# Mixture-of-experts stage of a fused attention and feed-forward kernel: separate weight signals, later shared additions, four result buffers and a split last gate-up

## The chip, the cores and the metric

One core of a Trainium2 chip runs the whole kernel in one launch. The metric is the device time of one execution in microseconds (us), as the median of several runs. Engines are named as the profile names them: PE (matrix products), ACT (scalar), DVE (vector), POOL (GpSimd) and SP (which issues most of the DMAs).

## What is computed

The kernel computes one transformer layer on 896 tokens (8 sequences of 112) of width 512, in fp32. After a cross-attention block (`x` becomes 896 x 512) comes a feed-forward block:

```python
x = hidden_states.reshape(T, H)
scores = jax.nn.softmax(x @ gate_weight.T, axis=-1)
topk_w, topk_idx = jax.lax.top_k(scores, 2)
combine = jnp.zeros((T, E)).at[jnp.arange(T)[:, None], topk_idx].add(topk_w)
gu = jnp.einsum('th,efh->tef', x, gate_up_weights)        # E = 8 experts, F = 352
act = silu(gu[..., :F]) * gu[..., F:]
y = jnp.einsum('tef,te,ehf->th', act, combine, down_weights)
sgu = x @ shared_gate_up.T                                 # shared expert, Fs = 704
y = y + (silu(sgu[:, :Fs]) * sgu[:, Fs:]) @ shared_down.T
```

The layer's input is added to both blocks' results. Only the two best experts of each token have a weight that isn't zero, so the kernel computes only those.

## The kernel before

**Products in three passes.** A precise fp32 product is made of fast passes: each operand is split into a rounded part `hi` (fp32r) and the remainder `lo`, and a product is hi x lo + lo x hi + hi x hi. ACT copies `hi` (helper `hi`, line 911 in the profile), DVE subtracts to get `lo` (helper `lo`, line 1186). For expert weights this is done anew for every tile, since the split copies of one expert only fit once.

**Shared expert.** It runs in steps j = 0 to 5 over the width Fs (128 columns a step, the last 64), each for tokens t = 0 (4 tiles of 128) and t = 1 (3 tiles). `shared_down` makes the product of one token tile in PSUM bank B, CC, D or A, and DVE adds each into `xres` (`add_shared`, line 1391, semaphore `sres`). The additions of the last step (j = 4, to which the product of step 5 has been added) are seven: four for t = 0, three for t = 1. They run beside the start of the expert stage.

**Routing.** DVE works out the slot of each (token, expert) pair; POOL scatters the rows to `xs_dram` so that each of 21 tiles of 128 rows belongs to one expert. `eid` holds each tile's expert, and every engine reads it with a register load (`value_load`) before it uses the expert's weights.

**Expert stage, tile i = 0 to 20.** In the order of each engine's own instruction list:

- SP: `load_x(i)` fetches the tile's rows to `xs_in` when PE has transposed the tile before (`Tx`). It also writes `xres` to `out` in two pieces (`start_sum`, line 362): tiles 0 to 4, and tiles 5 and 6 once all seven last additions are done. Both landings, with an older one, make `ysum0` reach 48. The lists of the weight DMAs are SP's too: 8 gate-up loads and the first down loads, signalled by `we`, and the last three experts' down loads, by `we_late`.
- PE: `gate_up(i)`, 24 products (line 837) in four chunks of the contraction; `t_x(i + 1)`, 4 transposes (line 737); `down(i - 1)`, 6 split products (line 524, semaphore `edn_split`) and the plain rest (line 854, `edn`); `t_act(i)`, 3 transposes of the activation (line 876). `down(i - 1)` waits for `ey` of the tile before it, as both use bank A. The last tile's down product (`last_down`, line 865) is plain, in two column parts.
- ACT: the next tile's first three `gu_hi`, `silu(i)`, `xs_hi(i + 1)`, the fourth `gu_hi`, `dn_hi(i)`, `put_y(i - 1)` (line 1116: bank A times the routing weight to `y_sb`), `put_actT(i)`. Before all this ACT waits for `we` and for the last shared gate-up. For the last tile the order is `silu`, `put_last_actT`, `put_y(19)`, `put_last_y`.
- DVE: two `gu_lo` of the next tile, `expert_act(i)` (line 1499), `xs_lo(i + 1)`, two more `gu_lo`, `dn_lo(i)`, `aT_lo(i)`; ahead of the loop the `gu_lo` of tile 0, each followed by one shared addition, then two more; the seventh addition follows in i = 0.
- POOL: `dn_hi1(i + 1)` (line 493: the second half of the down weights' `hi`, allowed once `edn_split` says that the earlier down product has read the buffer), then the scatter-add of tile i's result to `out` (line 505). Scatter i waits for `ey`, and for `yst` = 16 i, so for the landing of scatter i - 1; scatter 0 waits for `ysum0` = 48 as well. Two `y_sb` buffers: `put_y(i)` waits for the landing of scatter i - 2.

Of the kernel before, what the change touches and what calls it, by code (L numbers as in the profile page):

```python
# [5 lines left out]
ACT = mybir.ActivationFunctionType  # L6
# [6 lines left out]
P = 128  # L13
# [29 lines left out]
def build(nc, x, ctxT, wqT, wkvT, woT, gateT, guT, dnT, sguT, sdnT, out):  # L43
# [118 lines left out]
    actT_plain = m.inside(loop, "actT_plain", [P, P])  # L162
    act_last = nc.alloc_sbuf_tensor_at("act_last", [P, len(FK), P], F32, offset=x2T_at)
    y_sb = [m.inside(loop, f"y_sb{i}", [P, H]) for i in range(2)]

    parts = [shared_at, shared_end]
    gu_parts = m.inside(parts, "gu_parts", [P, C, 2, 2 * F], F32R)
# [56 lines left out]
    def ring_parts(b):  # L224
# [6 lines left out]

    names = (

        "x0 xt1 xt2 xrest wq0 wq1 wq2 wq3 wkeys wvals wo wgate ctx0 ctx1 wsg0 wsg1 wsd0 wsd1 wsd2 we we_late "

        "const zt sel zero wgpad sumg idf "

# [15 lines left out]
    with nc.Block() as block:  # L253
# [3 lines left out]
        def _(sp):  # L257
# [42 lines left out]
            def load_gu(e, sem):  # L300
                sp.dma_start(w_gu[:, e * GU:(e + 1) * GU], guT[e].rearrange("p c f -> p (c f)")).then_inc(sem, 16)
# [24 lines left out]
                sp.dma_start(xs_in[:, 0:H], xs_dram[bass.ds(i * P, P), 0:H]).then_inc(s["xin"], 16)  # L326

            for e in range(0, 2):
                load_gu(e, s["we"])
            next_sd(2)  # L330
            next_sg(2)
            for e in range(2, 5):
                load_gu(e, s["we"])
            next_sg(3)
            next_sd(3)
            for e in range(5, E):
                load_gu(e, s["we"])
            for e in range(n_early):
                load_dn(e, s["we"])
            next_sd(5)  # L340
            next_sg(4)
            next_sd(4)
# [4 lines left out]
            sp.wait_ge(s["ysum0"], 16)  # L347
            load_x(0)
            for e in range(n_early, E - n_late):
                load_dn(e, s["we"])  # L350
            sp.dma_start(dest[:, :, :], xs_dram[:, H:H + 2].bitcast(U32).rearrange("(n p) o -> p n o", p=P),
                         allow_slow_non_contiguous=True).then_inc(s["dest"], 16)
            sp.wait_ge(s["sg"], NBLK * NJ)
            for e in range(E - n_late, E):
                load_dn(e, s["we_late"])


            sp.wait_ge(s["Tx"], 1)
# [6 lines left out]
            start_sum(0, BLK + 1)  # L365
            sp.wait_ge(s["Tx"], 2)
            load_x(2)
            sp.wait_ge(s["sres"], NX * ND)
            start_sum(BLK + 1, NX)
            with sp.Fori(3, NT) as i:  # L370
                sp.wait_ge(s["Tx"], i)
                load_x(i)

# [5 lines left out]
        def _(pool):  # L379
# [102 lines left out]
            scatter(1, "scat2")  # L482

            pool.wait_ge(s["pos"], 3)
            pool.wait_ge(s["we"], 16 * (3 * E - 2 * n_late))
            pool.wait_ge(s["we_late"], 16 * 2 * n_late)
            pool.wait_ge(s["sdn"], NX * ND)

            def dn_hi1(i):
                e = pool.value_load(eid[0:1, i:i + 1], min_val=0, max_val=E - 1)  # L490
                if i >= 1:
                    pool.wait_ge(s["edn_split"], i)
                pool.tensor_copy(dn2[0][:, 1, :], w_dn[:, bass.ds(e * DN + H, H)]).then_inc(s["dn_hi1"], 1)  # L493

            dn_hi1(0)
            for i in range(NT):
                if i + 1 < NT - 1:
                    dn_hi1(i + 1)
                if i == 0:
                    pool.wait_ge(s["dest"], 16)  # L500
                    pool.wait_ge(s["ysum0"], 16 * 3)
                pool.wait_ge(s["ey"], i + 1)
                if i >= 1:
                    pool.wait_ge(s["yst"], 16 * i)
                pool.indirect_dma_start(  # L505
                    out=out[:, :], out_offset=bass.IndirectOffsetOnAxis(ap=dest[:, i, 0:1], axis=0),
                    in_=y_sb[i % 2][:, :], in_offset=None, compute_op=ALU.add).then_inc(s["yst"], 16)


        @block.tensor  # L510
        def _(pe):
# [372 lines left out]
            gate_up(1)  # L884
            t_x(2)
            pe.wait_ge(s["pos"], 3)
            pe.wait_ge(s["we"], 16 * (3 * E - 2 * n_late))
            pe.wait_ge(s["we_late"], 16 * 2 * n_late)
            down(0, expert(0))
            t_act(1)  # L890
            with pe.Fori(2, NT - 1) as i:
# [4 lines left out]
                down(i - 1, e)  # L896
                t_act(i)
            e_last = [expert(i) for i in (NT - 2, NT - 1)]
            gate_up(NT - 1)
            pe.wait_ge(s["ey"], NT - 2)  # L900
            down(NT - 2, e_last[0])
            t_act(NT - 1)
            fill_with_transposes(S[2], 5)
            pe.wait_ge(s["sres"], NX * ND)
            last_down(NT - 1, e_last[1])

# [2 lines left out]
        def _(act):  # L909
# [201 lines left out]
            def put_y(i):  # L1111

                act.wait_ge(s["edn"], i + 1)
                if i >= 2:
                    act.wait_ge(s["yst"], 16 * (i - 1))
                act.activation(y_sb[i % 2][:, :], A[:, :], ACT.Copy, scale=dest[:, i, 1:2].bitcast(F32))\  # L1116
                    .then_inc(s["ey"], 1)

            def put_last_y(i):
                act.wait_ge(s["yst"], 16 * (i - 1))  # L1120
                for n, (bank_, at, width) in enumerate(last_parts):
                    act.wait_ge(s["edn"], i + 1 + n)
                    ins = act.activation(y_sb[i % 2][:, at:at + width], bank_[:, 0:width], ACT.Copy,
                                         scale=dest[:, i, 1:2].bitcast(F32))
                ins.then_inc(s["ey"], 1)

# [8 lines left out]
                act.activation(actT_plain[0:w, :], B[0:w, 2 * P:3 * P], ACT.Copy).then_inc(s["aT"], 1)  # L1135

            act.wait_ge(s["pos"], 3)
            act.wait_ge(s["we"], 16 * (3 * E - 2 * n_late))

            act.wait_ge(s["sg"], NBLK * NJ)  # L1140
            e = expert(0)
# [3 lines left out]
            for i in range(NT):  # L1145
                if i + 1 < NT:
                    e_next = expert(i + 1)
                    for c in range(C - 1):
                        gu_hi(e_next, i + 1, c)
                if i == NT - 1:  # L1150
                    silu(i)
                    put_last_actT(i)
                    put_y(i - 1)
                    break
                silu(i)
                xs_hi(i + 1)
                gu_hi(e_next, i + 1, C - 1)
                if i == 0:
                    act.wait_ge(s["sdn"], NX * ND)
                    act.wait_ge(s["we_late"], 16 * 2 * n_late)  # L1160
                    act.wait_ge(s["dest"], 16)
                dn_hi(e, i)
                if i >= 1:
                    put_y(i - 1)
                put_actT(i)
                e = e_next
# [4 lines left out]
        def _(dve):  # L1171
# [333 lines left out]
            for c in range(C):  # L1505
                if c == 2:
                    xs_lo(0)
                gu_lo(e, 0, c)
                add_shared(ND - 1, 0, c, c + 1)
            add_shared(ND - 1, 1, 0, 2)  # L1510
            for i in range(NT):
                if i + 1 < NT:
                    e_next = expert(i + 1)
                    for c in range(2):
                        gu_lo(e_next, i + 1, c)
                expert_act(i)
                if i + 1 < NT:
                    xs_lo(i + 1)
                    for c in range(2, C):
                        gu_lo(e_next, i + 1, c)  # L1520
                    dn_lo(e, i)
                    aT_lo(i)
                else:
                    dve.wait_ge(s["Ta"], i + 1)
                    w = FK[2][1]
                    dve.tensor_copy(act_last[0:w, 2, :], B[0:w, 2 * P:3 * P]).then_inc(s["aT_last"], 1)
                if i == 0:
                    add_shared(ND - 1, 1, 2)
                e = e_next

# [33 lines left out]
```

## Time and profile before

| what | value |
|---|---|
| median of 3 runs | 351.81 us (350.88 to 352.39) |
| the profiled execution, its own time | 353.07 us |
| span of that profile | 351.3 us |
| PE busy | 332.9 us (95%) |
| DVE busy | 271.6 us (77%) |
| ACT busy | 230.0 us (65%) |
| POOL busy | 118.5 us (34%) |
| granted clock of PE, mean | 0.992 of full speed |

The profile is one execution. Times in it count from its first instruction. A timeline row gives start, duration, engine, line, operation, result <- operands, shape and count; in square brackets stands how long the engine had been idle before it, and which instruction (or DMA) ended that idle time. The chain of work that ended last is followed back from the last instruction, each step to what released it. "SPq", "ACTq" and the like are an engine's instruction queue, as opposed to its datapath. Busy times of matrix products are modelled at their ends, so consecutive rows of PE overlap a little: the distance between starts is what to read.

### The profile page before, as it was taken

How to read it: one execution, taken by the hardware profiler on the slowest of the kernel's cores; microseconds unless marked ns; L12 is line 12 of the kernel's file. 1: busy time of each engine (PE TensorE's matmuls, PEld its weight loads, DVE VectorE, ACT ScalarE, POOL GpSimd, SP SyncE). 2: the span in 40 equal slices, each digit the busy share in tenths (PEclk: the TensorE clock that was granted, in tenths of full speed). 3: DMA queues.
4: the chain of work that ended last, by engine and by line, in shares of the span. 5: the costliest groups of instructions: out<-in, count | busy, mean ns of one | idle time of the engine just before them, and what ended most of it. 6: DMA issues, size and time to landing. Idle time of an engine off the chain costs nothing.

```text
span 351.3 us, 7091 instructions
## 1 busy us (share of the span) xinstructions
PE 332.9 (95%) x2281; PEld 280.5 (80%) x2282; DVE 271.6 (77%) x464; ACT 230.0 (65%) x586; POOL 118.5 (34%) x136
## 2 busy tenths in 40 slices
PE   6999989999999999999999999999999999999980
PEld 6898877777776797988897878898889889988860
DVE  4798978999946258835586998999899899989900
ACT  3577899999973233213235578888888888888720
POOL 3332753555541000256200033343244234324411
PEclk9999999999999999999999999999999999999996
DMA  7999100000003799993599735434443543444233
GB/s 253 368 349 380 64 3 2 3 2 2 2 2 108 284 331 387 400 355 129 169 292 246 261 101 86 93 60 72 82 88 60 82 92 67 67 82 91 30 41 49
DMA packets 29051, 49.47 MB, mean 141 GB/s; under 512 B 7136, under 2 KB 12256, under 8 KB 28000
## 3 DMA queue, kind: packets, MB, share of 16 engines
q1 hardware_dynamic: 24880, 39.91, 35.0%
q0 software_dynamic: 4144, 9.23, 15.0%
q8 instruction: 13, 0.21, 0.3%
q14 instruction: 14, 0.11, 0.1%
HBM read 32.22 MB, written 16.92 MB: 140 GB/s over the span
## 4 chain that ended last, share of the span: by engine, by line
PE 54%; ACT 14%; DVE 10%; DMA 9%; issue 5%; POOL 4%; SPq 1%; POOLq 1%; ACTq 0%; DVEq 0%
PE bank L837 22%; PE bank L524 19%; ACT prob L956 8%; PE bank L854 5%; POOL xs_dram L474 4%; DMA xs_dram<-x2n,slot_i 3%; DMA w_dn<-dnT 3%; PE bank L708 2%; PE bank L876 2%; ACT probT L911 2%; PE bank L737 1%; DMA out<-y_sb,dest 1%; DVE xres L1391 1%; DMA w_sg<-sguT 1%; DMA ctx<-ctxT 1%
## 5 line engine op out<-in xcount | busy, mean ns | idle before, releaser
L1186 DVE TENSOR_TENSOR gu_parts<-w_gu,gu_parts 128x704 fp32r<-128x704 f32 x84 | 78.9, 972 | 1.7 <-ACT gu_parts L911 1.6
L911 ACT ACTIVATE gu_parts<-w_gu 128x704 fp32r x84 | 66.2, 794 | 18.4 <-PE bank L837 17.2
L837 PE MATMUL bank<-gu_parts,xsT_hi 128*128 128x352 f32 x336 | 69.5, 328 | 0.8 <-DVE xsT_lo L1186 0.8
L837 PEld LDWEIGHTS bank<-gu_parts,xsT_hi 128*128 128x128 f32 x336 | 55.6, 189 | 1.6 <-issue 1.2
L493 POOL CAST dn_hi<-w_dn 128x512 fp32r x20 | 19.7, 984 | 101.0 <-PE bank L524 69.0
L505 POOL DMA_INDIRECT out<-y_sb,dest x21 | 33.3, 1585 | 22.9 <-ACT y_sb L1116 17.2
L837 PE MATMUL bank<-gu_parts,xsT_lo 128*128 128x352 f32 x168 | 40.9, 325 | 0.0
L524 PE MATMUL bank<-x2T_hi,w_sg_lo 128*128 128x512 f32 (+1 forms) x88 | 32.6, 371 | 0.3
L524 PE MATMUL bank<-x2T_hi,w_sg_hi 128*128 128x512 f32 (+1 forms) x88 | 32.0, 363 | 0.0
L524 PE MATMUL bank<-x2T_lo,w_sg_hi 128*128 128x512 f32 (+1 forms) x88 | 31.9, 363 | 0.0
L837 PEld LDWEIGHTS bank<-gu_parts,xsT_lo 128*128 128x128 f32 x168 | 29.3, 189 | 0.0
L911 ACT ACTIVATE act_s_hi<-act_s 128x512 fp32r<-128x512 f32 (+1 forms) x10 | 5.8, 578 | 32.4 <-DVE act_s L1371 20.2
L474 POOL DMA_INDIRECT xs_dram<-x2n,slot_i x14 | 14.3, 1019 | 37.1 <-DVE eid L1471 33.1
L1186 DVE TENSOR_TENSOR dn_lo<-w_dn,dn_hi 128x1024 fp32r<-128x1024 f32 x20 | 24.6, 1228 | 0.8 <-POOL dn_hi L493 0.8
L956 ACT ACTIVATE prob<-score,negmax 112x112 f32<-112x112 f32 x64 | 24.1, 411 | 0.0
L956 ACT ACTIVATE prob<-bank,negmax 112x112 f32<-112x112 f32 x64 | 21.8, 363 | 1.9 <-DVE negmax L1231 1.9
L1391 DVE TENSOR_TENSOR xres<-xres,bank 128x512 f32<-128x512 f32 x35 | 22.0, 677 | 0.0
L854 PE MATMUL bank<-w_dn,actT_plain 96*128 x40 | 20.5, 592 | 0.0
L524 PEld LDWEIGHTS bank<-x2T_hi,w_sg_lo 128*128 128x128 f32 x88 | 16.5, 188 | 4.9 <-issue 2.5
L1499 DVE TENSOR_TENSOR act_e<-bank,silu_e 128x352 f32<-128x352 f32 x21 | 11.0, 523 | 11.8 <-ACT silu_e L1109 11.8
L911 ACT ACTIVATE probT<-bank 112x448 f32<-112x448 f32 x32 | 16.6, 554 | 3.9 <-PE bank L708 3.9
L404 POOL TENSOR_TENSOR prob<-prob,rrow 112x448 f32<-112x448 f32 x16 | 14.7, 931 | 11.7 <-DVE rrow L1235 11.7
(196 smaller groups left out, 804.9 us busy)
## 6 DMA issues: line engine op xcount, KB each, us to landing
w_gu<-guT SPq DMA_DIRECT2D x8, 1408.0 KB, 9.7
xs_dram<-no_row SPq DMA_DIRECT2D x1, 5460.0 KB, 19.2
xs_in<-xs_dram SPq DMA_DIRECT2D x21, 256.0 KB, 2.6
w_dn<-dnT SPq DMA_DIRECT2D x8, 512.0 KB, 6.2
w_sg<-sguT SPq DMA_DIRECT2D x10, 256.0 KB, 5.6
w_dn<-dnT SPq DMA_DIRECT2D x8, 192.0 KB, 6.7
w_sd<-sdnT SPq DMA_DIRECT2D x5, 256.0 KB, 4.8
out<-xres SPq DMA_DIRECT2D x1, 1280.0 KB, 5.4
```

Of the source, the lines that this page charges most:

```text
L404: pool.tensor_tensor(prob[r][:, :, :], prob[r][:, :, :], rrow[:, r, :].unsqueeze(2).to_broadcast([SQ, C, SQ]), ALU.mult)\
L474: pool.indirect_dma_start(out=xs_dram[:, :], out_offset=bass.IndirectOffsetOnAxis(ap=slot_i[:, k, n:n + 1], axis=0), in_=x2n[:, n, :], in_ ...
L493: pool.tensor_copy(dn2[0][:, 1, :], w_dn[:, bass.ds(e * DN + H, H)]).then_inc(s["dn_hi1"], 1)
L505: pool.indirect_dma_start(out=out[:, :], out_offset=bass.IndirectOffsetOnAxis(ap=dest[:, i, 0:1], axis=0), in_=y_sb[i % 2][:, :], in_offse ...
L524: ins = pe.matmul(dst, a, b, start=start and n == 0, stop=stop and n == len(passes) - 1)
L837: ins = pe.matmul(dst[:, 0:F], xsT[x_][:, c, :], gu2[w_][:, c, f0:f0 + F], start=c == 0 and n == 0, stop=c == C - 1 and n == 2)
L854: pe.matmul(A[:, :], actT_plain[0:w, :], w_dn[0:w, bass.ds(e * DN + 2 * H, H)], start=False, stop=True).then_inc(s["edn"], 1)
L911: act.activation(dst, src, ACT.Copy).then_inc(s[sem], 1)
L956: ins = act.activation(prob[r][:, c, :], src, ACT.Exp, bias=negmax[:, r, c:c + 1], accum_out=rowsum[:, r, c:c + 1])
L1186: dve.tensor_tensor(lo_, src, hi_.bitcast(F32), ALU.subtract).then_inc(s[sem], 1)
L1391: dve.tensor_tensor(xres[:, n, :], xres[:, n, :], (B, CC, D, A)[i][:, :], ALU.add)\
L1499: dve.tensor_tensor(act_e[:, :], S[1][:, 0:F], silu_e[:, :], ALU.mult).then_inc(s["eact"], 1)
```

## The change

1. The semaphores `we` and `we_late` become `wegu` (gate-up loads), `wedn` and `wedn_late` (down loads). ACT waits only for `wegu` ahead of the stage, and for the down loads ahead of its first `dn_hi`. POOL's wait for the down weights and the shared product moves behind its first register load.
2. DVE: ahead of the loop each shared addition comes before its `gu_lo`, not after it; one addition follows instead of two; the last two are made in i = 1 and i = 2, behind `aT_lo(i)`, instead of one in i = 0. SP's second `start_sum` moves behind `load_x(4)` accordingly.
3. Four `y_sb` buffers (the new two lie where `act_s0` was). POOL's list now runs `dn_hi1` two tiles ahead of the scatter for i below 4: dn 0, 1, 2, scatter 0, dn 3, scatter 1, dn 4, scatter 2, dn 5, scatter 3, scatter 4, dn 6, scatter 5, dn 7, and so on, one ahead.
4. Last tile: `gate_up(20)` is cut in two halves of two chunks with `down(19)` between them; 8 filling transposes follow it and 4 (before: 5) follow `t_act(20)`; ACT makes `put_y(19)` ahead of `silu(20)`.

```diff
@@ SP
-            for e in range(0, 2):
-                load_gu(e, s["we"])
+                load_gu(e, s["wegu"])
...
             for e in range(n_early, E - n_late):
-                load_dn(e, s["we"])
+                load_dn(e, s["wedn"])
...
-                load_dn(e, s["we_late"])
+                load_dn(e, s["wedn_late"])
...
             load_x(2)
+            for i in (3, 4):
+                sp.wait_ge(s["Tx"], i)
+                load_x(i)
             sp.wait_ge(s["sres"], NX * ND)
             start_sum(BLK + 1, NX)
-            with sp.Fori(3, NT) as i:
+            with sp.Fori(5, NT) as i:
@@ POOL
-            pool.wait_ge(s["we"], 16 * (3 * E - 2 * n_late))
-            pool.wait_ge(s["we_late"], 16 * 2 * n_late)
-            pool.wait_ge(s["sdn"], NX * ND)
             def dn_hi1(i):
                 e = pool.value_load(eid[0:1, i:i + 1], min_val=0, max_val=E - 1)
-                if i >= 1:
+                if i == 0:
+                    pool.wait_ge(s["wedn"], 16 * 2 * (E - n_late))
+                    pool.wait_ge(s["wedn_late"], 16 * 2 * n_late)
+                    pool.wait_ge(s["sdn"], NX * ND)
+                else:
                     pool.wait_ge(s["edn_split"], i)
...
             dn_hi1(0)
+            dn_hi1(1)
             for i in range(NT):
-                if i + 1 < NT - 1:
-                    dn_hi1(i + 1)
+                ahead = 2 if i < NY else 1
+                if i != NY and i + ahead < NT - 1:
+                    dn_hi1(i + ahead)
...
-                    in_=y_sb[i % 2][:, :], in_offset=None, compute_op=ALU.add).then_inc(s["yst"], 16)
+                    in_=y_sb[i % NY][:, :], in_offset=None, compute_op=ALU.add).then_inc(s["yst"], 16)
@@ PE
-            gate_up(NT - 1)
+            gate_up(NT - 1, range(C // 2))
             pe.wait_ge(s["ey"], NT - 2)
             down(NT - 2, e_last[0])
+            gate_up(NT - 1, range(C // 2, C))
+            fill_with_transposes(S[2], 8)
             t_act(NT - 1)
-            fill_with_transposes(S[2], 5)
+            fill_with_transposes(S[2], 4)
@@ ACT
-                if i >= 2:
-                    act.wait_ge(s["yst"], 16 * (i - 1))
+                if i >= NY:
+                    act.wait_ge(s["yst"], 16 * (i - NY + 1))
...
-            act.wait_ge(s["we"], 16 * (3 * E - 2 * n_late))
+            act.wait_ge(s["wegu"], 16 * E)
...
                 if i == NT - 1:
+                    put_y(i - 1)
                     silu(i)
                     put_last_actT(i)
-                    put_y(i - 1)
...
                     act.wait_ge(s["sdn"], NX * ND)
-                    act.wait_ge(s["we_late"], 16 * 2 * n_late)
+                    act.wait_ge(s["wedn"], 16 * 2 * (E - n_late))
+                    act.wait_ge(s["wedn_late"], 16 * 2 * n_late)
@@ DVE
+                add_shared(ND - 1, 0, c, c + 1)
                 gu_lo(e, 0, c)
-                add_shared(ND - 1, 0, c, c + 1)
-            add_shared(ND - 1, 1, 0, 2)
+            add_shared(ND - 1, 1, 0, 1)
...
-                if i == 0:
+                if i == 1:
+                    add_shared(ND - 1, 1, 1, 2)
+                if i == 2:
                     add_shared(ND - 1, 1, 2)
```

## Rows read from the trace of the kernel before

**Rows 1.** Chain of work that ended last, one tile of the expert loop.

```profile
214.97 3.89 PE bank L837 x24
...
219.15 1.47 PE bank L524 x6
...
221.81 3.89 PE bank L837 x24
```

**Rows 2.** The same chain, what it stands on where the stage starts.

```profile
178.32 9.49 DMA w_dn<-dnT
```

**Rows 3.** Timeline of ACT, start of the stage.

```profile
186.97 0.53 ACT L911 ACTIVATE act_p<-silu_s 64x384 fp32r<-64x384 f32 x1 [0.74 <-DVE silu_s L1371]
188.74 2.83 ACT L911 ACTIVATE gu_parts<-w_gu 128x704 fp32r x4 [1.25 <-DMA w_dn<-dnT]
...
198.08 0.47 ACT L1109 ACTIVATE silu_e<-bank 128x352 f32<-128x352 f32 x1
```

**Rows 4.** Timeline of PE, start of the stage.

```profile
190.47 0.46 PE L737 MATMUL bank<-ident_f,xs_in 128*128 128x128 f32 x4
191.44 0.47 PE L524 MATMUL bank<-w_sd_hi,act_s_lo 128*128 128x512 f32 x1 [0.51 <-DVE xres L1391]
...
194.00 0.81 PE L837 MATMUL bank<-gu_parts,xsT_hi 128*128 128x352 f32 x4
...
200.02 0.88 PE L837 MATMUL bank<-gu_parts,xsT_hi 128*128 128x352 f32 x4
...
207.91 0.89 PE L837 MATMUL bank<-gu_parts,xsT_hi 128*128 128x352 f32 x4 [0.77 <-DVE xsT_lo L1186]
```

**Rows 5.** Timeline of DVE, start of the stage.

```profile
198.81 0.51 DVE L1499 TENSOR_TENSOR act_e<-bank,silu_e 128x352 f32<-128x352 f32 x1
199.25 0.68 DVE L1186 TENSOR_TENSOR xsT_lo<-bank,xsT_hi 128x512 fp32r<-128x512 f32 x1
...
202.35 1.23 DVE L1186 TENSOR_TENSOR dn_lo<-w_dn,dn_hi 128x1024 fp32r<-128x1024 f32 x1 [0.83 <-POOL dn_hi L493]
...
203.82 0.68 DVE L1391 TENSOR_TENSOR xres<-xres,bank 128x512 f32<-128x512 f32 x1
```

**Rows 6.** Stretch of one tile: length; PE, PEld, DVE, ACT, POOL busy; clock, DMA.

```profile
214.74:221.57 6.83, 6.83 (x43) 6.00 (x40) 6.30 (x9) 5.75 (x11) 2.63 (x3) 1.00 0.44 77
```

**Rows 7.** Timeline of SP, the second write of xres.

```profile
204.53 0.39 SPq L362 DMA_DIRECT2D out<-xres x1
```

**Rows 8.** Timeline of POOL in the expert stage.

```profile
206.07 0.61 POOL L493 CAST dn_hi<-w_dn 128x512 fp32r x1 [3.87 <-PE bank L524]
208.29 1.94 POOL L505 DMA_INDIRECT out<-y_sb,dest  x1 [1.61 <-DMA out<-xres]
...
220.80 1.04 POOL L493 CAST dn_hi<-w_dn 128x512 fp32r x1 [3.56 <-PE bank L524]
...
332.06 1.56 POOL L505 DMA_INDIRECT out<-y_sb,dest  x1 [0.64 <-ACT y_sb L1116]
...
344.92 1.54 POOL L505 DMA_INDIRECT out<-y_sb,dest  x1 [4.13 <-DMA out<-y_sb,dest]
```

**Rows 9.** The instructions of line 505, their landings.

```profile
DMA to landing us min/median/max: 4.4/4.9/5.4
```

**Rows 10.** Chain of work that ended last, scatter 19.

```profile
339.24 4.93 DMA out<-y_sb,dest
```

**Rows 11.** Timeline of all engines, last two tiles.

```profile
331.09 0.69 ACT L1116 ACTIVATE y_sb<-bank,dest 128x512 f32<-128x512 f32 x1
...
331.30 0.88 PE L837 MATMUL bank<-gu_parts,xsT_hi 128*128 128x352 f32 x4
...
333.23 0.41 DVE L1186 TENSOR_TENSOR actT_split_lo<-bank,actT_split_hi 128x256 fp32r<-128x256 f32 x1
...
337.48 0.49 PE L876 MATMUL bank<-ident,act_e 128*128 128x128 f32 x3
...
340.86 0.98 ACT L1123 ACTIVATE y_sb<-bank,dest 128x384 f32<-128x384 f32 x2 [1.89 <-PE bank L865]
```

More of the change, by code:

```diff
@@ L164, in build @@
     y_sb = [m.inside(loop, f"y_sb{i}", [P, H]) for i in range(2)]
+    y_sb += [nc.alloc_sbuf_tensor_at(f"y_sb{i + 2}", [P, H], F32, offset=act0_at + 4 * H * i) for i in range(2)]
+    NY = len(y_sb)
     parts = [shared_at, shared_end]
@@ L232, in build @@
     names = (
-        "x0 xt1 xt2 xrest wq0 wq1 wq2 wq3 wkeys wvals wo wgate ctx0 ctx1 wsg0 wsg1 wsd0 wsd1 wsd2 we we_late "
+        "x0 xt1 xt2 xrest wq0 wq1 wq2 wq3 wkeys wvals wo wgate ctx0 ctx1 wsg0 wsg1 wsd0 wsd1 wsd2 wegu wedn wedn_late "
         "const zt sel zero wgpad sumg idf "
@@ L332, in _ @@
             for e in range(2, 5):
-                load_gu(e, s["we"])
+                load_gu(e, s["wegu"])
             next_sg(3)
@@ L336, in _ @@
             for e in range(5, E):
-                load_gu(e, s["we"])
+                load_gu(e, s["wegu"])
             for e in range(n_early):
-                load_dn(e, s["we"])
+                load_dn(e, s["wedn"])
             next_sd(5)
@@ L349, in _ @@
             for e in range(n_early, E - n_late):
-                load_dn(e, s["we"])
+                load_dn(e, s["wedn"])
             sp.dma_start(dest[:, :, :], xs_dram[:, H:H + 2].bitcast(U32).rearrange("(n p) o -> p n o", p=P),
@@ L886, in _ @@
             pe.wait_ge(s["pos"], 3)
-            pe.wait_ge(s["we"], 16 * (3 * E - 2 * n_late))
-            pe.wait_ge(s["we_late"], 16 * 2 * n_late)
+            pe.wait_ge(s["wedn"], 16 * 2 * (E - n_late))
+            pe.wait_ge(s["wedn_late"], 16 * 2 * n_late)
             down(0, expert(0))
@@ L1113, in put_y @@
                 act.wait_ge(s["edn"], i + 1)
-                if i >= 2:
-                    act.wait_ge(s["yst"], 16 * (i - 1))
-                act.activation(y_sb[i % 2][:, :], A[:, :], ACT.Copy, scale=dest[:, i, 1:2].bitcast(F32))\
+                if i >= NY:
+                    act.wait_ge(s["yst"], 16 * (i - NY + 1))
+                act.activation(y_sb[i % NY][:, :], A[:, :], ACT.Copy, scale=dest[:, i, 1:2].bitcast(F32))\
                     .then_inc(s["ey"], 1)
             def put_last_y(i):
-                act.wait_ge(s["yst"], 16 * (i - 1))
+                act.wait_ge(s["yst"], 16 * (i - NY + 1))
                 for n, (bank_, at, width) in enumerate(last_parts):
                     act.wait_ge(s["edn"], i + 1 + n)
-                    ins = act.activation(y_sb[i % 2][:, at:at + width], bank_[:, 0:width], ACT.Copy,
+                    ins = act.activation(y_sb[i % NY][:, at:at + width], bank_[:, 0:width], ACT.Copy,
                                          scale=dest[:, i, 1:2].bitcast(F32))
```

## The prediction

> **What bounds the kernel now.** I read the chain of waits first, then the timelines of the engines where the chain leaves PE. From tile 3 of the expert stage on the chain stands on PE alone [rows 1]: a gate-up of 3.89 us, from whose start it is 219.15 - 214.97 = 4.18 to the down product (gate-up and `t_x`), and 221.81 - 214.97 = 6.84 to the next gate-up. Over one tile PE is busy for all of 6.83 us, DVE for 6.30, ACT 5.75, POOL 2.63 [rows 6]. No edit shortens a product, so a gain can only come from the two ends of the stage.
>
> At its start the chain stands on the last early down-weight load, which lands at 178.32 + 9.49 = 187.81 [rows 2]; ACT issued its last shared piece at 186.97, and makes the first gate-up weights at 188.74 [rows 3]. PE then stands 0.51 us for DVE's first shared addition, and before gate-up 2, at 207.91, for DVE's `xsT_lo` [rows 4]. At the end two scatters run one after the other: scatter 19 starts at 339.24 and lands 4.93 us later [rows 10], scatter 20 starts at 344.92 [rows 8] and the span ends at 351.3, so 6.38 behind the last scatter's start.
>
> I call G(i) the start of gate-up i. Before: G(0) 194.00, G(1) 200.02, G(2) 207.91 [rows 4], G(20) 331.30 [rows 11].
>
> **Part 1, signals and additions: PE leads by 1.78 us at G(2).** ACT no longer waits for the down weights. Landing to first `gu_hi` was 188.74 - 187.81 = 0.93 (register load included); from the last shared issue at 186.97 that makes 187.90, 0.84 earlier [rows 2, 3]. The first addition no longer stands behind `gu_lo`, so it needs only PE's product, and PE runs on from 190.47 + 0.46 = 190.93 where it resumed at 191.44 [rows 4]. The addition that the next product needs, and `xs_lo(0)`, come forward with ACT's copies, so I carry the 0.51: G(0) = 193.49.
>
> G(1) waits for `xs_lo(1)`. `silu(0)` starts 198.08 - 194.00 = 4.08 behind G(0), so at 197.57; it takes 0.47. In the old run DVE was late to its `act_e` because of the additions ahead of it; now `act_e` can start at 198.08, 0.51 behind `silu`, and `xs_lo(1)` 199.25 - 198.81 = 0.44 later, at 198.52. From there to the gate-up was 200.02 - 199.25 = 0.77, so G(1) = 199.29, 0.73 earlier [rows 3, 4, 5].
>
> G(2) would have been 200.02 + 6.84 = 206.86 had nothing waited; it was 207.91, so 1.05 is the loss there. DVE was late through its wait of 0.83 for POOL's half of the weights, and the addition at 203.82, 0.68 long [rows 5]. POOL's register load now runs before its wait, and the addition is gone from this tile. Together with the 0.73 that is 2.2 us, more than the 1.05, so PE is not stopped: G(2) = 199.29 + 6.84 = 206.13, a gain of 1.78. The other bound is 0.51 alone (a second hold that I don't see takes the rest). I take 1.78, since each wait in it is named by a row.
>
> The two additions now fall in tiles where DVE is busy 6.30 of 6.83 [rows 6]. 0.53 is free, and an addition is 0.68 long with about 0.08 of overlap: 0.6. The excess of 0.07 twice is covered, as DVE's results lie ahead of their use: `aT_lo` starts 333.23 - 331.30 = 1.93 behind the gate-up start and is needed at 4.18 [rows 1, 11]. SP's two extra unrolled loads are the loop's own, and PE's split wait is for loads that landed before; both cost nothing. What `start_sum` at about 215.9 has behind it in SP's list, `load_x(5)`, is due only at G(3) + 4.18 = 217.2.
>
> **Part 2, the scatters start late, and POOL's list makes PE pay 2.12 us.** This is where I differ from what the four buffers seem to promise. Scatter 0 needs all of `xres` in `out`. The last addition was at 203.82, SP wrote at 204.53, scatter 0 began at 208.29: 4.47 behind the addition [rows 5, 7, 8]. Now the last addition comes behind `aT_lo(2)`: G(3) = 212.97, plus 1.93, plus 0.33 for `aT_lo` = 215.23. Scatter 0 starts at 219.70, 11.4 later.
>
> `yst` makes a scatter wait for the landing of the one before. Landing to next start was 344.92 - (339.24 + 4.93) = 0.75 [rows 8, 10]; a landing takes 4.9 in the median, 4.4 to 5.4 [rows 9]. I give the first 5.4, since it also issued for 1.94 and not 1.56 [rows 8], and the rest 4.9: scatter 1 at 225.85, then 5.65 each, 231.50, 237.15, and scatter 4 at 242.80, done issuing at 244.37. In PE's rhythm scatters are 6.84 apart, so the backlog shrinks by only 1.19 a tile and lasts until about scatter 10. `put_y` never waits for it: `put_y(4)`, at about 233, needs the landing of scatter 0 at 225.1.
>
> `dn_hi1` does wait. `dn 3` became ready at 220.80 [rows 8], now 1.78 earlier, 219.02, but stands behind scatter 0, until 221.64. It then meets an idle DVE and takes 0.61, as at 206.07, not 1.04 [rows 8]. `dn_lo` takes 1.14 up to the next start, `aT_lo` 0.41 [rows 11], so down 3 may run at 223.9; due is G(4) + 4.18 = 223.99. Not late, with 0.1 to spare. `dn 4` and `dn 5`, behind scatters 1 and 2, are ready when POOL is free within 1.6 us: covered. `dn 6` stands behind scatter 4: 244.37 + 0.05 + 0.61 + 0.05 + 1.14 + 0.41 = 246.63 for down 6, due at G(7) + 4.18 = 206.13 + 34.20 + 4.18 = 244.51. PE stands for 2.12 us. `dn 7`, behind scatter 5, is within its slack again.
>
> On the price of that cast: the steady one takes 1.04 beside a DVE subtraction [rows 8]. The Trainium skill (SBUF — State Buffer, "Who interferes with whom") says that a DVE instruction with two SBUF inputs and a GpSimd one that reads SBUF exclude each other in turn. The two durations agree with it; with 1.04 the stall would be 2.55.
>
> The unknown here is the scatters' spacing while they queue. From the shortest landing of 4.4, scatter 4 starts 1.5 earlier and 0.6 of the stall is left; from 5.4 for all, 3.6. I take the median row.
>
> **Part 3, the last tile: 1.10 us gained.** All is 0.34 late now (2.12 - 1.78): G(20) = 331.64. Two chunks take half of 3.89, but down 19 needs `aT_lo(19)`: 333.23 + 0.34 + 0.41 + 0.05 = 334.03, a stall of 0.44, better than the 3.89 that it waited for. Down 19 took 337.48 - (331.30 + 3.89) = 2.29 [rows 1, 11], so it ends at 336.32 and the second half at 338.27. `silu` starts 0.19 behind (4.08 - 3.89), 338.46; 0.51 later `act_e`, 0.51 long [rows 5]; 0.04 behind that `t_act(20)`: 339.52, where it was 337.48 [rows 11]. The eight transposes lie inside this wait. So the last result, ready at 340.86 + 0.98 = 341.84, comes 2.04 later, 343.88, and lets scatter 20 start 0.28 behind it (as 332.06 behind 331.09 + 0.69 [rows 8, 11]), at 344.16. The other input, scatter 19: y(19) would let it go at about 337.5, but scatter 18 starts at 332.06 + 0.34 [rows 8], lands 4.93 and lets go 0.75 later, 338.08; so scatter 20 could start at 343.76. The later one is 344.16, against 344.92 before: -0.76, of which this part is -1.10. Without the stall of part 2 it would be -2.88. Bounds of this part: nothing, if `put_y(19)` is late for a reason that I don't see, and 1.5 (to 343.76).
>
> **Sum.** -1.78 + 2.12 - 1.10 = -0.76. The profiled execution took 353.07, 1.26 above the median of the runs; what is added and taken away has the same length in both, so from 351.81 it is 351.0 us.
>
> **Rivals.**
> *The backlog costs nothing.* Landings queue closer than I read them, or POOL's late half is needed later. Then -2.88: 348.9; with 0.6 of stall left, 349.5. For it: only one pair of scatters back to back was traced. Against it: that pair measures 4.93 + 0.75, and it is the quiet end of the kernel. The Trainium skill (DMA: Bandwidth & Descriptors, "Anatomy of one DMA") gives a GpSimd-issued DMA 2.0 us plus its bytes at 436 GB/s, an estimate of 2.6 us for 256 KB; by that rule the backlog would be gone by scatter 3 and this rival would hold. The traced 4.9 speaks against it. 29%.
> *The late start costs twice, and the change is slower.* At `dn 3` I have 0.1 us to spare. If the second write of `xres` and what follows takes longer than 4.47, each us of it stops PE at down 3, while the stall at down 6 remains, since both its times move along. Slower by over 0.5% needs 2.6 us there: scatter 0 at 222.3. At 3 us the sum is -0.76 + 2.9 = +2.1: 353.9. For it: POOL's wait for that write was the only one it had, and the loads of rows share the queue. Against it: the write is smaller than the first piece, and alone. 9%.
> *The front gains less*, 0.51 only: +0.5, 352.3. Part of my case's range.
>
> **How the numbers follow.** 0.5%, about what a measurement of this kernel can tell from no change, is 1.76 us. My forecast, a mid-stage stall between 1.1 and 3.6 and a front gain between 0.5 and 1.8, has 62% and gives 350.0 to 352.6; it lies within 0.5% nearly wholly. Faster takes the first rival and the edge of mine: 0.31. Slower 0.09, same 0.60. The range reaches down to the case without a stall, 348.8, and up to 352.9.
>
> **What would show it.** Right: G(2) near 206.1, no PE wait by DVE there; scatter 0 at 219 to 220; scatters 5.65 apart until about scatter 9; one PE gap of about 2 us before down 6, with DVE's `dn_lo` waiting for POOL; down 19 between the halves, scatter 20 released by ACT. Wrong: no gap near 244 (first rival); a gap near 224 as well (second); G(2) later than 207.

## The result, and the profile after

The changed kernel takes 356.06 us in the median of 4 runs (355.38 to 356.13), the kernel before 351.96 (350.88 to 352.39) beside it: ratio 1.0108, 95% interval 1.0079 to 1.0137. It is slower by 4 us where I forecast 0.8 us less, and it lies outside my range of 348.8 to 352.9.

First the waits in the expert stage of the changed kernel: who waited for what, in total us, how often, and the longest.

```profile
POOL out L513 <- DMA out<-y_sb,dest: 23.9, 8, 4.1
...
POOL out L513 <- DMA out<-xres: 6.4, 1, 6.4
...
DVE dn_lo L1197 <- POOL dn_hi L499: 5.8, 2, 3.6
...
PE bank L845 <- issue: 2.4, 4, 1.0
```

Eight scatters waited for the landing of the one before, where only the last did before, and DVE waited 5.8 us in two places for POOL's half of the down weights. The timeline of POOL gives the order (answers to [rows 8]; line 513 is the scatter, 499 the cast `dn_hi1`):

```profile
212.04 1.12 POOL L499 CAST dn_hi<-w_dn 128x512 fp32r x1 [5.60 <-PE bank L532]
219.57 2.31 POOL L513 DMA_INDIRECT out<-y_sb,dest  x1 [6.41 <-DMA out<-xres]
221.28 1.21 POOL L499 CAST dn_hi<-w_dn 128x512 fp32r x1
225.70 1.59 POOL L513 DMA_INDIRECT out<-y_sb,dest  x1 [3.20 <-DMA out<-y_sb,dest]
...
231.41 1.58 POOL L513 DMA_INDIRECT out<-y_sb,dest  x1 [2.90 <-DMA out<-y_sb,dest]
...
237.78 2.04 POOL L513 DMA_INDIRECT out<-y_sb,dest  x1 [2.85 <-DMA out<-y_sb,dest]
243.90 1.55 POOL L513 DMA_INDIRECT out<-y_sb,dest  x1 [4.08 <-DMA out<-y_sb,dest]
244.89 1.19 POOL L499 CAST dn_hi<-w_dn 128x512 fp32r x1
```

`dn 3` runs behind scatter 0, at 221.28; `dn 6` behind scatter 4, at 244.89. On DVE the two that wait for them:

```profile
222.64 1.23 DVE L1197 TENSOR_TENSOR dn_lo<-w_dn,dn_hi 128x1024 fp32r<-128x1024 f32 x1 [2.27 <-POOL dn_hi L499]
...
246.22 1.23 DVE L1197 TENSOR_TENSOR dn_lo<-w_dn,dn_hi 128x1024 fp32r<-128x1024 f32 x1 [3.56 <-POOL dn_hi L499]
```

And PE (answers to [rows 4]; line 845 is the gate-up, 745 the transposes `t_x`, 532 the down product):

```profile
189.74 0.46 PE L745 MATMUL bank<-ident_f,xs_in 128*128 128x128 f32 x4
...
192.38 0.80 PE L845 MATMUL bank<-gu_parts,xsT_hi 128*128 128x352 f32 x4
...
197.16 0.54 PE L745 MATMUL bank<-ident_f,xs_in 128*128 128x128 f32 x4 [0.82 <-DMA xs_in<-xs_dram]
...
227.83 0.89 PE L845 MATMUL bank<-gu_parts,xsT_hi 128*128 128x352 f32 x4 [0.61 <-issue]
...
247.98 0.47 PE L532 MATMUL bank<-dn_hi,actT_split_lo 128*128 128x512 f32 x1 [1.25 <-DVE dn_lo L1197]
251.76 0.88 PE L845 MATMUL bank<-gu_parts,xsT_hi 128*128 128x352 f32 x4 [0.96 <-issue]
```

"issue" as the end of an idle time means that the profile shows no instruction and no DMA that PE waited for. What stood there is the matter of e3.

To compare kernels I cut each profile at the transposes `t_x`, one set per tile: from t_x(0) to t_x(3) is the stage's start, from t_x(3) to t_x(20) the middle (17 tiles, 116.3 if nothing waits), from t_x(20) to the end of the span the end. What differs before t_x(0) is not the change's: that code is the same, yet t_x(0) falls between 189.3 and 191.7 us in these profiles. Each row is one profiled execution; the ratio is of many runs. us:

| kernel | start | middle | end | ratio to before, 95% interval |
|---|---|---|---|---|
| before | 21.39 | 116.41 | 23.03 | |
| changed | 20.20 | 122.03 | 22.23 | 1.0108 (1.0079 to 1.0137) |
| e1 additions early | 20.17 | 117.57 | 22.07 | 1.0008 (0.9984 to 1.0032) |
| e2 two ahead up to 11 | 21.71 | 118.87 | 22.15 | 1.0045 (1.0021 to 1.0069) |
| e3 register load later | 20.78 | 121.91 | 22.51 | 1.0126 (1.0090 to 1.0163) |
| e4 last tile only | 21.15 | 116.21 | 22.28 | 0.9992 (0.9968 to 1.0016) |
| e5 early, one ahead | 19.89 | 116.43 | 22.42 | 0.9969 (0.9950 to 0.9989) |
| e6 e5 and rows first | 25.56 | 116.37 | 22.12 | 1.0115 (1.0097 to 1.0133) |
| e8 e6 and register later | 24.65 | 116.27 | 22.24 | 1.0083 (1.0059 to 1.0108) |
| e9 e5 and register later | 19.46 | 116.28 | 22.11 | 0.9939 (0.9913 to 0.9964) |
| e10 signals only | 20.03 | 116.41 | 22.54 | 0.9988 (0.9967 to 1.0009) |

The start ends behind G(2). The changed kernel gains 1.19 there and 0.80 at the end and loses 5.62 in the middle: +3.6, where the medians lie 4.1 apart. The other 0.5 us is less than what executions of one kernel differ by (the profiled execution of before took 353.07 where its median is 351.96), and how much one row of this table can be off by is seen in e4 and e10. The loss has an address. Distances between successive `t_x`, read from the timelines of PE, us:

| from, to | 4, 5 | 5, 6 | 6, 7 | 7, 8 | 8, 9 | 9, 10 | 10, 11 |
|---|---|---|---|---|---|---|---|
| before | 6.84 | 6.84 | 6.84 | 6.94 | 6.87 | 6.84 | 6.84 |
| changed | 6.83 | 8.05 | 7.40 | 7.10 | 9.44 | 7.60 | 7.10 |
| e1 | 6.93 | 6.88 | 6.83 | 6.84 | 7.43 | 7.52 | 6.83 |
| e2 | 6.84 | 8.05 | 6.83 | 7.00 | 6.87 | 7.19 | 6.84 |
| e3 | 6.84 | 7.40 | 6.84 | 6.84 | 11.92 | 6.83 | 6.84 |
| e5 | 6.85 | 6.84 | 6.84 | 6.95 | 6.87 | 6.83 | 6.85 |

The stretch 5, 6 holds down 3, which needs `dn 3`, and 8, 9 holds down 6. Over 6.84, the first group of three stretches loses 1.21 + 0.56 + 0.26 = 2.03, the second 2.60 + 0.76 + 0.26 = 3.62.

### The profile page after: what moved, and what is told of

Its sections match the earlier page's. It is cut to its first block, busy times and chain, and to the rows that moved or that the text cites. A ratio compares the mean times of both kernels' runs of the same rounds, so it can differ in the third digit from the quotient of the medians.

```text
span 354.2 us, 7094 instructions
## 1 busy us (share of the span) xinstructions
PE 335.3 (95%) x2288; PEld 282.7 (80%) x2289; DVE 272.6 (77%) x464; ACT 230.9 (65%) x586; POOL 121.8 (34%) x136
## 4 chain that ended last, share of the span: by engine, by line
PE 60%; ACT 12%; DMA 12%; DVE 7%; issue 5%; POOL 1%; POOLq 1%; SPq 0%; DVEq 0%
PE bank L532 32%; PE bank L845 16%; ACT prob L966 8%; DMA out<-y_sb,dest 7%; PE bank L862 4%; DMA xs_in<-xs_dram 2%; PE bank L716 2%; ACT probT L921 2%; PE bank L884 1%; PE bank L745 1%; DMA w_sg<-sguT 1%; DVE prob L1250 1%; DVE xnT_lo L1197 1%; DMA ctx<-ctxT 1%; DMA out<-xres 1%
## 5 line engine op out<-in xcount | busy, mean ns | idle before, releaser
L513 POOL DMA_INDIRECT out<-y_sb,dest x21 | 35.0, 1665 | 45.6 <-DMA out<-y_sb,dest 23.9
L499 POOL CAST dn_hi<-w_dn 128x512 fp32r x20 | 23.0, 1151 | 78.3 <-PE bank L532 48.8
L532 PE MATMUL bank<-dn_hi,actT_split_lo 128*128 128x512 f32 x40 | 17.3, 434 | 1.8 <-DVE dn_lo L1197 1.2
## 6 DMA issues: line engine op xcount, KB each, us to landing
xs_dram<-no_row SPq DMA_DIRECT2D x1, 5460.0 KB, 19.2
```

The costliest lines, as they stand in the source:

```text
L513: pool.indirect_dma_start(out=out[:, :], out_offset=bass.IndirectOffsetOnAxis(ap=dest[:, i, 0:1], axis=0), in_=y_sb[i % NY][:, :], in_offs ...
L532: ins = pe.matmul(dst, a, b, start=start and n == 0, stop=stop and n == len(passes) - 1)
```

## Experiments

### e1: the last additions back in their old places

```diff
-            add_shared(ND - 1, 1, 0, 1)
+            add_shared(ND - 1, 1, 0, 2)
...
-                if i == 1:
-                    add_shared(ND - 1, 1, 1, 2)
-                if i == 2:
+                if i == 0:
                     add_shared(ND - 1, 1, 2)
```

SP's second `start_sum` goes back behind `load_x(2)`.

> The changed kernel with one part undone: the last shared additions are made where the kernel before made them (two ahead of the loop, the seventh in tile 0), and SP writes the second piece of xres before it fetches row tile 3. Theory (the late additions hold scatter 0 back, and POOL's in-order list then hands PE its down weights late at down 3 and down 6, which costs 5.6 us by the trace): scatter 0 starts near 208, no DVE wait for POOL's half of the weights beyond tile 0, G(20) - G(2) = 18 x 6.84 = 123.1 instead of 128.9, and with the addition back in tile 0 G(2) up to 1 us later; in all 5 to 5.6 us less than the changed kernel, so 350.5 to 351.1. Rival (the four result buffers or the list two ahead cost by themselves, by their order or by the shared SBUF ports, and the additions don't matter): 355 to 356.

352.42 us where before takes 352.23. Most of the loss is gone: the late additions cause it, and the four buffers don't. But it isn't all gone, the time lies above the 350.5 to 351.1 that I expected, and scatter 0 isn't at 208. The timeline of POOL in e1:

```profile
213.05 1.06 POOL L496 CAST dn_hi<-w_dn 128x512 fp32r x1 [5.83 <-PE bank L529]
214.27 2.08 POOL L510 DMA_INDIRECT out<-y_sb,dest  x1 [0.16 <-issue]
```

SP wrote `xres` at its old time, but in the list two ahead `dn 2` stands in front of scatter 0, and it waits for PE's down 1. So scatter 0 is held twice in the changed kernel, once by the additions and once by the list; with only the second left, it is one tile late, scatters still queue up (240.78 is scatter 4), and DVE waits 1.38 us for `dn 6`. Of the 1.3 us lost in stretches 8 to 10, the 0.59 of the first follow from that wait; the 0.68 of the second stand behind a register load of PE that took 1.02 us (of which in e3). My theory had missed the second hold.

### e2: two ahead for longer

```diff
-                ahead = 2 if i < NY else 1
-                if i != NY and i + ahead < NT - 1:
+                ahead = 2 if i < 12 else 1
+                if i != 12 and i + ahead < NT - 1:
```

> The changed kernel, with POOL's list two tiles ahead up to scatter 11 instead of scatter 3, so that no half of the down weights stands behind the queue of scatters until the backlog has shrunk. Theory (the switch from two ahead to one ahead, dn 6 behind scatter 4, costs 3.65 us in tiles 7 to 10; dn 3 behind scatter 0 costs the other 2.06): the stop before down 6 is gone, the one before down 3 stays, so 3.0 to 3.7 us less than the changed kernel: 352.4 to 353.1. Rival A (the stop only moves to the new switch, since one tile ahead again meets late scatters): 355 to 356.5, with a PE gap in tiles 14 to 16. Rival B (the backlog is no cause at all): no change, 356.

353.55, 2.5 us under the changed kernel and not the 3.0 to 3.7 that I expected. The stop at down 6 is gone and the one at down 3 stays at 8.05, as the theory has it; in the profiles the middle is 3.16 us shorter. But the start of this execution is 1.51 longer, as it stood 2.37 us ahead of t_x(1), of which below. Rival A is there too, in small: `dn 14`, behind scatter 12, starts at 299.08, DVE's `dn_lo` waits 1.38 us for it, and stretch 16 to 17 takes 7.16. Stretch 18 to 19 takes 7.22, behind a register load of 0.72 us.

### e3: PE's register load behind the gate-up

```diff
-                e = expert(i - 1)
                 gate_up(i)
+                e = expert(i - 1)
```

> The changed kernel, with PE's register load of the expert number moved in the loop from ahead of the gate-up to behind it (it is first used by the down product). The trace of the changed kernel shows four gate-ups that start 0.34 to 0.96 us after everything they need, put down to issue, each right behind a late activation. Theory (the register load can be queued only once the late activation has come, so it stands open ahead of the gate-up): these gaps of 2.4 us in all shrink to under 0.5, the gate-ups of tiles 5 and 8 start directly behind their transposes, and the kernel takes 1.2 to 2.4 us less: 353.7 to 354.9. Rival (the gaps belong to the late xsT_lo and its weight load, not to the register): no change, 355.7 to 356.4.

356.28: no gain at all, and yet each gap put down to issue ahead of a gate-up is gone from tiles 4 to 9 (stretch 5, 6 is 7.40 and not 8.05; 6, 7 and 9, 10 are clean). So the gaps were the register load's, and they had two causes. Two of them, 0.61 ahead of G(5) and 0.96 ahead of G(8), are as my theory has it: the activation came late, and the load, which stands behind PE's wait for it, began only then (at 226.8, where PE's `t_act` is at 226.72; in a steady tile it begins at 218.7 and `t_act` is at 219.51). At the other two, 0.34 ahead of G(6) and 0.53 ahead of G(9), no activation was late: `t_act` came 6.57 us behind the gate-up's start, as in every tile. There the load itself was long. PE's register loads in the changed kernel at these two places (ns min, median, max; start of the first and last):

```profile
L850 PEldq TENSOR_LOAD <-eid x1: 932/932/932, 233.5 to 233.5; - x1
L850 PEldq TENSOR_LOAD <-eid x1: 1088/1088/1088, 257.5 to 257.5; - x1
```

In the kernel before none takes over 0.32 us from tile 2 on. My theory had all four gaps behind late activations, which is wrong for two. Either way the load is hidden once it stands behind the gate-up.

But PE reached down 6 earlier and stood there longer. The timeline of PE in e3, then its stretches (length; busy time of PE, PEld, DVE, ACT, POOL; granted clock; DMA):

```profile
244.84 0.45 PE L745 MATMUL bank<-ident_f,xs_in 128*128 128x128 f32 x4
248.70 0.57 PE L532 MATMUL bank<-dn_hi,actT_split_lo 128*128 128x512 f32 x1 [3.41 <-DVE actT_split_lo L1197]
249.07 0.63 PE L532 MATMUL bank<-dn_lo,actT_split_hi 128*128 128x512 f32 x1
249.50 0.63 PE L532 MATMUL bank<-dn_hi,actT_split_hi 128*128 128x512 f32 x1
```

```profile
244.84:248.70 3.86, 0.45 (x5) 0.34 (x4) 1.56 (x2) 1.73 (x4) 1.95 (x2) 1.00 0.55 114
248.70:252.60 3.90, 3.90 (x8) 2.48 (x9) 3.84 (x6) 0.63 (x1) 2.02 (x2) 0.56 0.13 24
252.60:256.70 4.10, 4.10 (x28) 4.07 (x27) 3.90 (x5) 3.31 (x6) 0.69 (x2) 1.00 0.52 66
```

Down 6 is pinned by scatter 4 (it starts at 244.62 here, 243.90 in the changed kernel), so what PE saves ahead of it is waited out at it. And there is a price on top: after 3.41 us of idle time PE has a granted clock of 0.56 in the next 3.9 us (0.50, its 1.2 GHz level, from 250 to 252), and the products follow at 0.43 us and not 0.23. From down 6 to the next gate-up it takes 252.87 - 248.70 = 4.17 us, where a steady tile of the kernel before takes 221.57 - 218.99 = 2.58. So of the 2.2 us of gaps that the changed kernel has behind down 6, 0.7 are saved: from down 6 to t_x(11) it is 21.73 us and not 22.44. These 0.7 are lost again since scatter 4, and down 6 with it, came 0.72 later in this execution. The open load is real, but up to down 6 it isn't the cause of the loss.

### e4: the last tile's part alone

The kernel before with the fourth edit of the change only.

> The kernel before, with only the last tile's part of the change: the last gate-up in two halves with down 19 between them, 8 and 4 filling transposes, and put_y(19) ahead of silu(20). Theory: scatter 19 starts 1.3 to 1.5 us sooner and scatter 20, released by ACT and no longer by the landing of scatter 19, 0.85 us sooner, as in the changed kernel: 0.7 to 1.1 us less than the kernel before, 350.9 to 351.3. Rival (the last product ends later by as much as the scatters gain, so nothing is left): no change, 351.7 to 352.1.

351.62 against 352.23, ratio 0.9992: by the runs not to be told from no change, by the profile 0.75 us shorter at the end (22.28 for 23.03). Counted from t_x(20), scatter 19 starts after 337.12 - 327.82 = 9.30 us (before 339.24 - 328.27 = 10.97) and scatter 20 after 15.81 (before 16.65). The size is what I expected, at the limit of what the runs can show, and part of it is the luck of one row: see e10.

### e5: early additions, and one ahead throughout

e1, and:

```diff
             dn_hi1(0)
-            dn_hi1(1)
             for i in range(NT):
-                ahead = 2 if i < NY else 1
-                if i != NY and i + ahead < NT - 1:
-                    dn_hi1(i + ahead)
+                if i + 1 < NT - 1:
+                    dn_hi1(i + 1)
```

> The changed kernel with the last additions and SP's second write as before, and POOL's list one tile ahead throughout, as before; the separate weight signals, the addition before each gu_lo, four result buffers and the split last tile stay. Theory (scatter 0 was held twice, by the late additions and, with those undone, by dn 2 ahead of it in the list, which left it at 214.3 us and cost a rest of 1.3 us in tiles 7 and 8): scatter 0 starts near 207 to 208.5, no PE stop from tile 3 to tile 19 (17 x 6.84 us), the end 0.75 us shorter than before, the start 0 to 1 us shorter: 350.4 to 351.5 where the kernel before takes 352.2. Rival (the rest in tiles 7 and 8 belongs to the four buffers or to DVE): stops remain, 352 or more.

351.1 where before takes 352.37, ratio 0.9969 (0.9950 to 0.9989): faster than both kernels. Scatter 0 is released by ACT and no longer by the write of `xres`, the middle is 116.43, no stop. From the timeline of POOL in e5:

```profile
206.17 2.58 POOL L508 DMA_INDIRECT out<-y_sb,dest  x1 [1.60 <-ACT y_sb L1121]
```

With both holds on scatter 0 gone, nothing of the loss is left, and the gains of the start (1.5) and the end (0.6) stand.

The fourth corner, late additions with the list one ahead, can't be run: scatter 0 would wait for an addition that DVE makes behind `dn_lo(2)`, and the cast for that would stand behind scatter 0. So the list two ahead isn't a choice beside the late additions, it is forced by them.

### e6 and e8: row tile 1 ahead of the late down weights

```diff
-            for e in range(E - n_late, E):
-                load_dn(e, s["wedn_late"])
             sp.wait_ge(s["Tx"], 1)
             load_x(1)
+            for e in range(E - n_late, E):
+                load_dn(e, s["wedn_late"])
```

> As e5_one_ahead_adds_early, and SP fetches row tile 1 ahead of the last three experts' down weights instead of behind them. Theory (in the changed kernel PE stands 0.8 to 2.4 us ahead of its second transposes because that fetch takes 6.9 us in the company of those loads, and this is what eats the gain at the start): the fetch takes 2.6 to 4 us, the wait is gone, G(1) comes 0.8 us or more sooner after the first transposes than in e5; total 0.5 to 1 us less than e5. Rival (the down weights then land late, and ACT's dn_hi(0) and with it down 0 and tile 1 wait for them by as much): no difference to e5 or slower, with a PE stop ahead of down 0.

> As e6_rows_first, with PE's register load behind the gate-up in the loop. Theory (the register load stands open only where an activation comes late, and with the scatters in time only tile 2 can have that): at G(2) up to 0.8 us sooner where the activation is late, nothing anywhere else; total 0 to 0.8 us less than e6. Rival (the load stands open in each tile once it is placed there, ahead of the transposes): 0.3 us or more lost in each tile, 5 us slower.

356.41 and 355.59. The fetch of tile 1 is quick (2.8 us) and its wait is gone: t_x(0) to t_x(1) stays 6.44, as in e5. But the loads, now later, meet the write of `xres` and the next fetch. The timelines of SP and then of PE in e6:

```profile
191.00 0.34 SPq L328 DMA_DIRECT2D xs_in<-xs_dram  x1
...
193.84 0.48 SPq L310 DMA_DIRECT2D w_dn<-dnT  x1
195.69 0.39 SPq L362 DMA_DIRECT2D out<-xres  x1
197.38 0.34 SPq L328 DMA_DIRECT2D xs_in<-xs_dram  x1
```

```profile
205.32 0.61 PE L738 MATMUL bank<-ident_f,xs_in 128*128 128x128 f32 x4 [2.21 <-DMA xs_in<-xs_dram]
206.80 0.77 PE L525 MATMUL bank<-dn_hi,actT_split_lo 128*128 128x512 f32 x1 [0.87 <-issue]
```

Row tile 2, issued at 197.38, lands after 7.9 us; PE waits 2.21 and then 0.87 (there its register load, 0.80 long, stands open behind the late transposes), and again its clock falls: 1.00 up to 205.3, 0.73 from there to 206, 0.50 from 206 to 212. The rival won, and the wait that stopped PE was another than I named, the fetch of tile 2. The one that I named is there too, hidden behind it: ACT's `dn_hi(0)` waits 3.06 us for the weights, `aT_lo(0)` ends at 204.18, and down 0 was due at about 203.25. e8 against e6 is 0.9 us shorter at the start, and the middle isn't longer (116.27 and 116.37): a register load between gate-up and transposes is hidden in all tiles.

### e9: the register load behind the gate-up, on e5

> As e5_one_ahead_adds_early, and PE's register load behind the gate-up in the loop. Theory (in e5 the second gate-up of the loop's first round starts 0.5 us late, behind the open register load, and nothing else is left between tile 3 and tile 19): that 0.5 us goes and each further tile keeps 6.84 us; total 0.3 to 0.6 us less than e5, about 0.45% under the kernel before, with an interval that excludes no change. Rival (the late fetch of row tile 1 or 2 sets the start, so PE only waits elsewhere): no difference to e5.

349.68 where before takes 351.89, ratio 0.9939 (0.9913 to 0.9964): the lowest ratio of the study. The one gap left in e5, 0.34 us ahead of G(2), is gone, and t_x(2) to t_x(3) is 6.96 where e5 has 7.39. What did nothing in e3 pays here, since nothing behind it is pinned. The profiles account for 0.43 us at this place and 0.15 in the middle. The ratios differ by more, 0.30% or 1.1 us, but their intervals overlap; that e9 beats e5 at all is shown by the gap that is gone, and not by the runs.

### e10: the signals alone

The kernel before with the first edit (and four buffers, used as two were), without the new order of additions and without the split last tile.

> The kernel before, with only the separate weight signals, POOL's register load ahead of its wait, and four result buffers that are used as the two were (one tile ahead). Theory: this is most of the gain at the start; from the first transposes (t_x 0) to the fourth (t_x 3) it was 21.4 us before, 20.2 in the changed kernel and 19.9 in e5, and becomes 20.3 to 20.8 here; no stops in tiles 4 to 9; total 0.6 to 1.1 us less than the kernel before. Rival (the order of additions and weight copies on DVE made the gain, not the signals): 21.2 us or more from first to fourth, total unchanged.

351.48 against 351.89, ratio 0.9988 (0.9967 to 1.0009), unclear by the runs alone and less than the 0.6 to 1.1 us that I expected. The profile has 20.03 us from t_x(0) to t_x(3), 1.36 under before. The order of additions adds at most the 0.14 to e5, and e1, which has that order as well, has 20.17. So the first edit made most of the start's gain, as far as one profile of each can show it: e4, whose start is that of the kernel before, has 21.15, so a start without it varies by 0.24 at least.

The end of e10 tells something about e4. It lacks the split last tile, and is 0.49 us shorter than before's all the same. Scatter 20 there waits for the landing of scatter 19, which took 4.48 us and not 4.93, and starts 16.21 us behind t_x(20), where before has 16.65. In all nine kernels with the split last tile it starts at 15.79 to 15.83. So the split is worth 0.4 to 0.9 us, by how long that landing takes, and the trace of before showed the upper end.

## Why the prediction was wrong

**What held.** Scatter 0 at 219.57 (forecast 219.70), a queue of scatters behind it, `dn 6` stuck behind scatter 4, and DVE's `dn_lo` waiting for POOL there: the mechanism and its place are as forecast, e2 and e5 show it by removal. G(2) stands at 205.98 (forecast 206.13), but that is luck: two errors nearly cancel, below.

**What failed: the size of part 2's stall, 2.12 us in the sum, 5.62 measured.** The two gains were also smaller than forecast, 1.19 for 1.78 and 0.80 for 1.10, which is 0.9 us of the error; the other 3.5 are this one term. Three steps of it:

- *Scatter spacing.* I took 5.4 once and 4.9 after that. The scatters of tiles 0 to 9 (the first, the eight that waited behind it, and one in rhythm again) landed as follows (one profile, min, median, max):

```profile
DMA to landing us min/median/max: 4.6/5.2/5.8
```

  Scatters 0 to 3 took 5.4, 5.0, 5.6 and 5.4 to land, so the starts are 6.13, 5.71, 6.37 and 6.12 apart, and scatter 4 started at 243.90 and not 242.80. The median of scatters in rhythm was the wrong row for scatters that queue; why those land later was not tried. Down 6 ran at 247.98, not 246.63.
- *`dn 3` had 0.1 us to spare, and it cost 2.03.* Scatter 0 issued for 2.31, not 1.94; its cast ended at 222.49, not 222.25, and down 3 started at 224.40, 0.4 late. The other 1.6 us is the next point.
- *What comes behind a late value.* I let PE go on at once when the late value came. But DVE's whole list was late, so the activation of the tile was, and behind its wait stand PE's register load and the gate-up. This is the issue gap of 0.61 and 0.96 in the rows of PE above. That the gaps are the register load's is shown by e3 and e9, where they vanish. Perhaps my own [rows 4] had it, 0.77 ahead of G(2), which I put down to `xsT_lo`; on the kernel before this was not tried. The rest, 0.56 + 0.26 in stretches 6 to 8 and 0.76 + 0.26 in 9 to 11, lies behind register loads that were themselves long (0.93 and 0.46, 1.09 and 0.62 us). From tile 4 on such loads stand only in the changed kernel, e1 and e2, in the part where scatters queue, so they seem to belong to the backlog; what makes them long stays open.

e3 limits the weight of the last two: down 6 is pinned, so of the loss up to there, 3.6 us (due 205.98 + 5 x 6.84 + 4.18 = 244.36, measured 247.98), nothing could be saved by a quicker PE. Only scatter 4 counts for it. Behind it come 2.0 us more, which had no term in my sum: the gap ahead of G(8), and the two long loads.

**The cast's price was right.** `dn 3` ended 0.61 behind the end of its scatter (219.57 + 2.31 = 221.88, 221.28 + 1.21 = 222.49), `dn 6` 0.63 (245.45, 246.08), each with an idle DVE; the 1.04 of the steady tile would have been wrong. The rule of the Trainium skill (SBUF — State Buffer, "Who interferes with whom") agrees.

**The rule on a scatter's cost was wrong for this one.** The Trainium skill (DMA: Bandwidth & Descriptors, "Anatomy of one DMA") gives an estimate of 2.6 us for 256 KB; this indirect, accumulating DMA took 4.4 to 5.4 in rhythm [rows 9] and up to 5.8 while queued. My first rival, that the backlog costs nothing, rested on it in part. By that estimate the backlog would be gone at scatter 4, not at scatter 3 as I wrote: with 2.6 + 0.75 from start to start scatter 3 starts at 229.75, where the rhythm, 1.78 ahead of before's 229.33, has it at 227.55.

**The second rival** was the nearest: the late start costs at down 3 and again at down 6, and makes the kernel slower. I gave it 9%, and asked for scatter 0 at 222.3. It needs no such delay, as 0.1 us of slack was none. Its sum was wrong too: it adds the loss at down 3 to the one at down 6, but the 2.0 us lost around down 3 only made PE come later to a stop that scatter 4 had set.

**Part 1.** Behind t_x(0), G(2) came 1.20 earlier (205.98 - 189.74 against 207.91 - 190.47), not 1.78; that G(2) still stands near 206.1 is owed to t_x(0), which fell 0.73 sooner in this execution. G(0) gained 0.89 (2.64 against 3.53), more than my 0.51. Then t_x(1) waited 0.82 for row tile 1, a fetch that takes 6.9 us beside the late down weights. I had called the loads covered without asking when the next row tile lands. In e5 the fetch was in time, and the start gained 1.50. The late additions themselves cost PE next to nothing, as forecast: t_x(2) to t_x(3) takes 6.83, t_x(3) to t_x(4) 6.96.

**Part 3.** From G(20) to the end 19.2 us instead of 20.0: 0.8, forecast 1.10. The last result came at 346.51 + 0.98 = 347.49, 12.48 behind G(20), and I had 12.24; ACT released scatter 20, as forecast. How much that gains depends on the landing that the kernel before waits for there (e10), and I had one row of it.

## What to carry to other kernels

A queue in program order ties together things that have nothing to do with each other: whoever delays the first entry of a serial chain (here an accumulating scatter that must wait for its predecessor's landing) delays every other job in that list, so follow the list, not the buffers; four result buffers didn't help while casts for PE stood between the scatters. A slack of 0.1 us in a forecast should be priced as a stop, and a stop can cost more than its length, as the register loads and waits behind it come late too (here down 3 was 0.4 late and stretch 5, 6 lost 1.21). And before polishing the work ahead of a wait, look whether that wait is pinned from elsewhere: e3 saved nothing, e9 with the same edit did.

## What the hardware showed

- **The granted clock of PE.** After 3.41 us of idle time PE ran at 0.56 for 3.9 us (e3). In e6, after a gap of 2.21 us, the clock fell while four transposes ran (0.73) and was 0.50 through a second gap of 0.87 and the work behind it, up to 212. A gap of 2.37 us ahead of t_x(1) in e2, with work at full clock on both sides, cost none (1.00 after it), nor did the 1.25 us in the changed kernel.
- **A scatter's landing** took 4.4 to 5.4 us in rhythm [rows 9], and 4.7 to 5.8 (median 5.4) in scatters 0 to 8 of the changed kernel, which followed one another directly. What makes the difference was not tried.
- **PE's register load** takes 0.30 to 0.32 us in the rhythm of before; in the changed kernel single ones took 0.93 and 1.09 us (at 233.5 and 257.5). Behind the gate-up neither cost anything (e3, e8, e9).
- **SP's issue of the first late down load** took 1.40 us before, and 0.37 to 3.47 in other executions of the same list, which moves all that SP issues behind it: in e2, where it took 3.47, t_x(1) waited 2.37 us. It may be one source of the 2 to 3 us between executions of one kernel; why it varies was not tried.
